# Two graph layers over an 8192 x 8192 adjacency: 89 of its 256 blocks multiplied with seven half-size products instead of eight, VectorE making the combinations of their quarters

## The reference

```
h = relu(layernorm(x));  x = x + adj @ (h * (u >= 0.1) / 0.9)
h = relu(layernorm(x));  x = x + adj @ (h @ W) + b
```

## Time and profile before

| what | value |
|---|---|
| median of three runs | 919.41 us |
| profiled execution, its own device time | 920.12 us |
| profiled execution, span of the page | 918.3 us |
| TensorE matmul busy | 900.0 us, 98% |
| VectorE busy | 234.5 us, 26% |
| GpSimd busy | 2.6 us |
| transfers | 363.53 MB, mean 396 GB/s |
| granted TensorE clock | full speed in every slice |

### The profile page before, as it was taken

The page is one execution under the profiler, slowest core; times in us unless marked ns, Lnnn a source line. Parts: engine busy times, 40 slices in busy tenths (PEclk is TensorE's granted clock), DMA queues, the critical chain, the costliest instruction groups (busy, mean ns, idle before and its releaser), DMA issues.

```text
span 918.3 us, 10443 instructions
## 1 busy us (share of the span) xinstructions
PE 900.0 (98%) x4488; PEld 415.4 (45%) x4488; DVE 234.5 (26%) x449; ACT 42.8 (5%) x120; POOL 2.6 (0%) x13
## 2 busy tenths in 40 slices
PE   6799999999999999999999999999999999999998
PEld 5445444444444444444444444444444444444443
DVE  5364732323203202030303021030220300300334
ACT  3100000000000000000000000000000000000000
POOL 1000000000000000000000000000000000000000
PEclk9999999999999999999999999999999999999999
DMA  8999999999999999999999999989999999999993
GB/s 348 421 420 420 422 420 422 420 421 421 421 420 421 420 421 420 421 419 421 403 419 379 410 367 380 399 339 369 385 353 382 371 386 419 390 390 389 412 422 149
DMA packets 52909, 363.53 MB, mean 396 GB/s; under 512 B 5728, under 2 KB 6016, under 8 KB 10752
## 3 DMA queue, kind: packets, MB, share of 16 engines
q1 hardware_dynamic: 52800, 362.83, 97.5%
q0 software_dynamic: 64, 0.03, 0.0%
HBM read 360.74 MB, written 2.10 MB: 395 GB/s over the span
## 4 chain that ended last, share of the span: by engine, by line
PE 92%; DMA 5%; SPq 2%; issue 0%; DVE 0%
PE banks L720 45%; PE row_sums L695 37%; PE banks L714 6%; DMA blocks<-in_adj 5%; PE banks L730 3%; SPq L464 1%; PE row_sums L704 1%; PE banks L807 0%; PE finished L772 0%; PE row_sums L772 0%; SPq L447 0%; SPq L446 0%; DVE x L654 0%
## 5 line engine op out<-in xcount | busy, mean ns | idle before, releaser
L720 PE MATMUL banks<-blocks,features 128*64 128x512 f32 x1912 | 665.2, 593 | 0.0
L695 PE MATMUL row_sums<-blocks,features 128*64 128x512 f32 x1696 | 547.1, 592 | 1.5 <-DMA blocks<-in_adj 1.5
L720 PEld LDWEIGHTS banks<-blocks,features 128*64 128x64 f32 x1912 | 221.3, 137 | 215.6 <-issue 215.1
L695 PEld LDWEIGHTS row_sums<-blocks,features 128*64 128x64 f32 x1696 | 192.7, 137 | 201.6 <-issue 196.4
L617 DVE TENSOR_TENSOR acc<-acc,banks 64x512 f32<-64x512 f32 (+1 forms) x112 | 76.8, 686 | 597.9 <-PE banks L720 540.7
L714 PE MATMUL banks<-blocks,features 128*64 128x512 f32 x224 | 98.1, 592 | 0.1
L524 ACT ACTIVATE turned<-finished 32x128 f32<-32x128 f32 (+1 forms) x68 | 17.8, 262 | 790.3 <-DVE finished L584 789.1
L730 PE MATMUL banks<-blocks,features 128*64 128x256 f32 x240 | 54.3, 379 | 0.1
L714 PEld LDWEIGHTS banks<-blocks,features 128*64 128x64 f32 x224 | 30.6, 137 | 29.0 <-issue 28.8
L730 PEld LDWEIGHTS banks<-blocks,features 128*64 128x64 f32 x240 | 32.8, 137 | 21.7 <-issue 8.5
L704 PE MATMUL row_sums<-blocks,features 128*64 128x256 f32 x256 | 30.5, 382 | 7.1 <-DMA blocks<-in_adj 7.1
(11 more groups left out here) (48 smaller groups left out, 97.0 us busy)
## 6 DMA issues: line engine op xcount, KB each, us to landing
blocks<-in_adj SPq DMA_DIRECT2D x339, 1024.0 KB, 13.0
out<-x SPq DMA_DIRECT2D x7, 256.0 KB, 3.6
x<-in_x SPq DMA_DIRECT2D x1, 1024.0 KB, 10.9
acc<-in_u SPq DMA_DIRECT2D x1, 1024.0 KB, 12.9
blocks<-in_adj SPq DMA_DIRECT2D x2, 512.0 KB, 25.1
x<-in_x SPq DMA_DIRECT2D x1, 768.0 KB, 7.2
acc<-in_u SPq DMA_DIRECT2D x1, 768.0 KB, 8.8
x<-in_x SPq DMA_DIRECT2D x1, 256.0 KB, 3.1
```

Of the source, the lines that this page charges most:

```text
L695: return nc.tensor.matmul(row_sums[at, t.unit % 2, nodes], features[:, tile_of(k, j), 0:D], tile, start=first and t.n == unit_first[t.unit ...
L720: return nc.tensor.matmul(banks[at, t.sum.bank, nodes], features[:, tile_of(t.k, j), D:2 * D], tile, start=t.n == t.sum.first and j == t.t ...
```

## The change

From row 4 on, a `both` item becomes a **seven**: 89 of the 92. The 512 x 512 block A is seen as four quarters (2 halves of its nodes x 2 halves of its tiles) and the features as B with two halves of tiles x two layers. The 2 x 2 product A B then takes seven products of quarters instead of eight (Winograd's form), each of 2 matmuls of 256 columns: 14 matmuls of 256 in place of 8 of 512.

For that, combinations must be made first. VectorE makes four of features (`mixed`, 128 x 128 elements each) and four of quarters of the block (`quarters`, 128 x 512 elements each; one of them, A11 - A21, is written over A21 in the block's own slot), eight subtractions or additions per block, in `make_quarters`. There are two sets of these buffers, so a block's combinations may start when the seven before the last is used, and are placed at most three items ahead. The products of a whole row add up in two further PSUM banks; when the row's last seven is done, `add_seven` adds them to `x1` and `acc` in seven additions where there was one. A unit's end now waits for these.

The rest follows from it. The PSUM tensor `finished` goes, and the transposes of a unit's end are put into `row_sums` instead, so the first item of unit m waits for the copies out of it. The ring has 15 slots in place of 16. Loads of a seven are issued as if they were needed two items sooner. `merged` gives each queue a window: sevens start 12 us after a unit's begin and end 8 us before its end, late items lie between 14 us after the begin and 30 us before the end. The late `both(k + 1, k)` is put ahead of the pairs in `late`. `x` and `u` come in two parts instead of three.

```
-SLOTS = 16
+SLOTS = 15
+SEVEN_FROM = 4
+SEVEN_LOAD, SEVEN_MADE, SEVEN_SETS = 2, 3, 2
+SUM_BANKS, SEVEN_BANKS = 4, 2
-STEP, BLOCK_LOAD, LANDING, MARGIN, H2_LEAD, ROW_LEAD = 0.858, 2.49, 1.6, 8.0, 8.0, 10.0
-PARTS = [(0, 1), (1, 4), (4, PAIRS)]
+STEP, BLOCK_LOAD, LANDING, MARGIN, H2_LEAD, SEVEN_OFF, LATE_OFF = 0.858, 2.49, 1.6, 8.0, 8.0, (12.0, 8.0), (14.0, 30.0)
+PARTS = [(0, PAIRS // 2), (PAIRS // 2, PAIRS)]
...
     def both(self, s, k):
-        return Item("both", [self.operand(s, k)], k, s, s + 1)
+
+        whole = s < SEVEN_FROM or (s, k) == (BLOCKS - 1, BLOCKS - 2)
+        return Item("both" if whole else "seven", [self.operand(s, k)], k, s, s + 1)
...
+    for n, t in enumerate(sevens):
+        t.nth, t.set = n, n % SEVEN_SETS
+        t.at = max(t.n - SEVEN_MADE, t.loads()[0].released, sevens[n - SEVEN_SETS].n if n >= SEVEN_SETS else 0)
...
+            def make_quarters(t):
...
+                dve.wait_ge(h2_ready, t.needs)
+                if t.nth >= SEVEN_SETS:
+                    dve.wait_ge(used, sevens[t.nth - SEVEN_SETS].n + 1)
+                nc.vector.tensor_tensor(t1, b12, b11, ALU.subtract).then_inc(seven_mixed, 1)
+                nc.vector.tensor_tensor(t3, b22, b12, ALU.subtract).then_inc(seven_mixed, 1)
+                dve.wait_ge(seven_mixed, 4 * t.nth + 1)
+                nc.vector.tensor_tensor(t2, b22, t1, ALU.subtract).then_inc(seven_mixed, 1)
+                dve.wait_ge(seven_mixed, 4 * t.nth + 3)
+                nc.vector.tensor_tensor(t4, b21, t2, ALU.subtract).then_inc(seven_mixed, 1)
+                s1, s2, s4 = (quarters[:, t.set, n, :, :] for n in range(3))
+                dve.wait_ge(block_arrived[t.loads()[0].slot], t.loads()[0].arrived)
+                nc.vector.tensor_tensor(s1, a21, a22, ALU.add).then_inc(seven_made, 1)
+
+                nc.vector.tensor_tensor(a21, a11, a21, ALU.subtract).then_inc(seven_made, 1)
+                dve.wait_ge(seven_made, 4 * t.nth + 1)
+                nc.vector.tensor_tensor(s2, s1, a11, ALU.subtract).then_inc(seven_made, 1)
+                dve.wait_ge(seven_made, 4 * t.nth + 3)
+                nc.vector.tensor_tensor(s4, a12, s2, ALU.subtract).then_inc(seven_made, 1)
...
+                pe.wait_ge(seven_mixed, 4 * t.nth + 4)
+                for j in range(2):
+                    product(A11_B11, a11, b11, j, first=True)
+                    of_layer_1(1, 1, a22, t4, j)
+                for j in range(2):
+                    of_layer_1(j, 0, a12, b21, j)
+                pe.wait_ge(seven_made, 4 * t.nth + 2)
+                for j in range(2):
+                    product(S1_T1, s1, t1, j, first=True)
+                    product(S3_T3, s3, t3, j, first=True)
+                pe.wait_ge(seven_made, 4 * t.nth + 4)
+                for j in range(2):
+                    product(S2_T2, s2, t2, j)
+                    done = product(S4_B22, s4, b22, j)
```

More of the change, by code:

```diff
@@ L80, in __init__, with merged @@
     def __init__(self, p, half, n):
-        self.p, self.half, self.first, self.ahead = p, half, n, None
+        self.p, self.half, self.first, self.ahead, self.seven = p, half, n, None, None
 def stays(i, k):
     return k <= i // 2 * 2 + 1 + KEPT
-def merged(queues, lead):
+def merged(queues, windows):
     total = sum(t.steps * STEP for q in queues for t in q)
@@ L96, in merged @@
                 continue
[L97 to L101, removed]
+            begin, end = windows[n][0], max(total - windows[n][1], windows[n][0] + 1.0)
+            if now < begin and any(d < len(r) and now >= w[0] for d, r, w in zip(done, queues, windows)):
+                continue
+            at = begin + (end - begin) * (done[n] + 0.5) / len(q)
             if best is None or at < best[0]:
@@ L149, in layer_2_of @@
             late[-1].k1 = other.k
+        if 0 < k < BLOCKS - 1:
+            late.append(self.both(k + 1, k))
         for p in range(PAIRS - 1, -1, -1):
@@ L229, in items @@
                 again = again[:max(0, int((0.97 * work - loads) / (2 * BLOCK_LOAD - 4 * STEP * 0.97)))]
-                items += merged([both, ones, again, late], ROW_LEAD)
+                items += merged([both, ones, again, late], [SEVEN_OFF, (0, 0), (0, 0), LATE_OFF])
             self.waiting = [w for w in self.waiting if w[1] not in again]
@@ L245, in plan @@
             load.until = n
+    sevens = [t for t in items if t.kind == "seven"]
+    loads.sort(key=lambda load: load.first - (SEVEN_LOAD if items[load.first].kind == "seven" else 0))
     free, holder, count = [-1] * SLOTS, [None] * SLOTS, [0] * SLOTS
-    for load in loads:
+    for n, load in enumerate(loads):
         load.slot = min(range(SLOTS), key=lambda q: free[q])
-        assert free[load.slot] < load.first, "a block needs a slot that is still held"
+        assert free[load.slot] < min(later.first for later in loads[n:]), "a block needs a slot that is still held"
         count[load.slot] += 1
@@ L259, in plan @@
             for half in range(2):
-                if t.kind == "one" or (t.kind == "both" and half != t.row % 2) or (t.kind == "mix" and half == 1):
+                if t.kind in ("one", "seven") or (t.kind == "both" and half != t.row % 2) \
+                        or (t.kind == "mix" and half == 1):
                     unit_items[t.unit][half].append(n)
-    unit_first = {m: [h[0] for h in halves] for m, halves in unit_items.items()}
-    unit_last = {m: [h[-1] for h in halves] for m, halves in unit_items.items()}
+    unit_first = {m: {half: h[0] for half, h in enumerate(halves) if h} for m, halves in unit_items.items()}
+    unit_last = {m: {half: h[-1] for half, h in enumerate(halves) if h} for m, halves in unit_items.items()}
+    unit_end = {max(t.n for t in items if t.unit == m): m for m in range(UNITS)}
     sums, row_sum = [], {}
@@ L302, in plan @@
         bank_free[q.bank], bank_of[q.bank] = q.last, q
-    unit_end = {max(last): m for m, last in unit_last.items()}
     pair_end = {}
@@ L308, in plan @@
     finals = sorted(range(PAIRS), key=lambda p: pair_end[p])
-    return items, loads, sums, ahead_done, unit_first, unit_last, unit_end, pair_end, finals
+    return items, loads, sums, sevens, ahead_done, seven_done, unit_first, unit_last, unit_end, pair_end, finals
 def bass_gnn(nc, x, adj, u, wb, out):
@@ L314, in bass_gnn @@
     ALU, ACT, AX = mybir.AluOpType, mybir.ActivationFunctionType, mybir.AxisListType
-    items, loads, sums, ahead_done, unit_first, unit_last, unit_end, pair_end, finals = plan()
+    (items, loads, sums, sevens, ahead_done, seven_done, unit_first, unit_last, unit_end, pair_end,
+     finals) = plan()
     closing = {q.last: q for q in sums}
@@ L658, in _ @@
                 if n in closing:
-                    add_sum(closing[n])
+                    (add_sum if closing[n].seven is None else add_seven)(closing[n])
+                for t in sevens:
+                    if t.at == n:
+                        make_quarters(t)
                 if n - 1 in unit_end:
```

148 lines of the change are left out of this document (106 added, 42 removed).

## The result

The changed kernel takes 905.52 us, median of 4 runs (903.23 to 906.49), against 919.47 us for the kernel before beside it: a ratio of 0.9841, 95% interval 0.9829 to 0.9853, 14 us less. The forecast was 893 us with a range of 883 to 908. So the direction and the range held, and nearly half of the forecast gain of 26 us is missing. (A slot of `blocks` is 8 KB per partition, 4 tiles of 512 fp32 numbers, and not the 16 KB stated above.)

A forecast was written before the change was run, and what follows sets the result against it. TensorE's work, 98% busy, was taken to bound the kernel. From 919.4 us, 28.2 us saved after 450 us gave 891.2; 2 us added for VectorE in runs of sevens made 893 us, range 883 to 908.

The forecast's parts named there:

- TensorE's work: In each seven: seven couples of 256-column matmuls take 3.02 us against 3.43, saving 36.4 us over 89 blocks.
- Up to unit 9's end the saving is lost: Units 5 to 9, transfers full: their 20 sevens' 8.2 us counted as lost to waits for blocks.
- above the floor, so this saving is paid in full: After 450 us: 69 sevens save 28.2 us, span ends at 890 us, above a transfer floor near 875.
- The fourth rival: After 450 us: transfers become the bound, no gain, chance 0.03; a part, blocks late, 3 to 5 us, 897, chance 0.08.
- the smaller ring: SyncE's loads issued behind a slot's release come late by one slot, 2.5 us, counted inside the 8.2 us.
- the forecast's own case: Whole kernel: 893 us, own range 885 to 898, chance 0.52.
- the first rival: VectorE's combinations run at full length, 4.18 us per seven: 10.5 us more, 902 us (898 to 906), chance 0.17.
- the second: TensorE runs dry at sevens' new waits, 0.22 us each time: 908 us, twice 923 (900 to 923), chance 0.12.
- VectorE: In make_quarters: eight operations overlap to 3.5 us per seven, VectorE about 70% busy; 2 us added for runs of sevens.
- TensorE empties at its new waits: At a seven's waits, though VectorE is in time: 0.22 us once each, 15 us over 69 sevens; chance 0.12.
- Slower by VectorE's operations on blocks: VectorE's operations on blocks cost more than any row shows: slower from 4.6 us per seven, 925 us and more; chance 0.08.
- The unit's end at nothing: Row's end additions (4.2 us) and the unit's own chain (6.3 us) cost nothing, as nobody waits before late begins.

The follow-up runs named there:

- e7: The changed kernel with its order and 15 slots, but all 92 blocks as boths with eight products and no combinations: 923.30 us.
- e2: The changed kernel with a ring of 14 slots in place of 15, nothing else: 934.86 us.
- e4: The changed kernel with loads of sevens issued in plain order of first use, not two items sooner: 896.47 us.
- e6: The changed kernel with 16 slots, room coming from two shared buffers, so the right value of one product is left out: 893.70 us.
- e9: The changed kernel, 15 slots, loads in plain order of first use and other windows for sevens and late items: 889.94 us.
- e10: The order of e9 with the 16 slots and two shared buffers of e6, one product's right value left out: 887.91 us.
- e5: The changed kernel with four more waits, so each of a seven's eight VectorE operations waits for the one before it: 910.61 us.
- e1: The changed kernel with VectorE's four combinations of quarters made for only 64 of their 512 elements: 902.74 us.

## Why the prediction was half right

- *TensorE's work.* 3.02 us per seven, 36.4 us in all: measured at 3.02. Right.
- *Up to unit 9's end the saving is lost.* 8.2 us forecast. Where unit 9 ends is told by ScalarE's operation of the earlier trace rows; in the change it is

```profile
439.16 0.30 ACT L585 ACTIVATE dev<-square,eps 128x4 f32<-128x4 f32 x1 [1.21 <-DVE square L652]
```

| kernel | slots | unit 9's end, us | from there to the end of the span, us |
|---|---|---|---|
| before | 16 | 447.5 | 470.9 |
| e7 (eight products) | 15 | 450.0 | 470.9 |
| the change | 15 | 439.2 | 464.2 |
| e2 | 14 | 444.1 | 489.9 |
| e4 | 15 | 438.8 | 456.2 |
| e6 | 16 | 439.2 | 453.1 |
| e9 | 15 | 437.7 | 450.8 |
| e10 | 16 | 437.8 | 448.6 |

  By unit 9's end the order of the sevens has done two pairs less than the kernel before (163 loads, not 167), 6.9 us of work. With nothing saved it would end at 440.6 us; it ended at 439.2, so 6.8 of the 8.2 us were lost. No order and no 16th slot of these runs brings it below 437.7. Right in mechanism and size.
- *"above the floor, so this saving is paid in full".* This is the step that failed. I set the bytes left after 450 us against the full rate and found a floor of 875 us, 15 us under the time so far. A floor from the mean rate says nothing on single blocks: the ring has 15 slots, the late blocks landed 7.3 to 10.2 us after issue, and the order gave some of them 5.2 us. Beyond unit 9's end the sum gives 470.9 + 6.9 - 28.2 = 449.6 us; measured are 464.2, so 14.6 of the 28.2 us were not paid. TensorE stood still for 9.2 us more than before from 450 us to the end, and two stretches at half clock cost 2 x 1.7 us; some 2 us are not placed. The fourth rival named it ("a block late here and there") and undersized it, at 3 to 5 us. I had put the smaller ring into 2.5 us inside the 8.2, where e2 and e6 show 29 and 12 us per slot. That the ring, the order and the early loads make the loss is shown: each was changed by itself (the ring in e2 and e6, the loads in e4, the order in e9 against e4), and e9 brings this part to 450.8 us. How the rest divides between the order and the sevens' pace is not shown beyond what e7 says.
- *The range.* It held by width and not by its reasons. 905.5 lies outside the 885 to 898 of the forecast's own case and above the fourth rival's 895 to 902. It lies in the ranges of the first rival (898 to 906) and the second (900 to 923), and neither of these happened: the time alone would have pointed to the wrong cause.
- *VectorE.* Pitch 3.50 forecast, 3.48 measured; waits of TensorE for it 0.8 us, 2 us allowed, and at the end of unit 16 as said. The rival at full length was priced at 10.5 us, 9 of it above the forecast; by hand (e5) it is 5 us on top of the late blocks. Right, but for some 4 us that e1 leaves open.
- *TensorE empties at its new waits.* A seven without late operands runs in 3.02 us; the rival is out.
- *Slower by VectorE's operations on blocks.* They last 684 to 692 ns; out.
- *The unit's end at nothing.* TensorE's wait for features written there was 1.0 us, once. Right.

What stays open: how the 7.3 to 10.2 us from issue to landing divide into waiting behind other loads and the block's own transfer; how much of the run-to-run spread of the change (3.3 us; the kernel before had 0.5 us beside it and 4.4 us beside e1 to e4) is the clock; and the 4 us of e1.

## What to carry to other kernels

A floor of bytes by the mean rate is necessary and not sufficient: in a ring, ask of each load which item frees its slot and how much work lies between that item and the use, and hold it against the time from issue to landing, not against the pitch. When a change makes the consumer faster, that distance shrinks, and one slot or an "earlier" load, which holds a slot longer, can cost more than the new work: 12 us and 9 us here, against 3 to 4 us that came back with most of VectorE's (e1). Keep items with two loads apart in the order, and price a wait of TensorE with the clock that it may cost after it.

## What the runs showed that I had not expected

- Issuing loads earlier made blocks later: 9 us (e4).
- A wait of 2.3 us and one of 3.5 us of TensorE were each followed by a stretch at half clock of 3.4 us; the wait of 3.0 us that ended near 255 us was followed by none in the change (clock 1.00), and by one in e1 and e6 (0.60 from 254.4 to 258.2 us in e1, 0.67 from 254.9 to 258.5 in e6). So the length of the wait alone doesn't decide.
- One slot beside fifteen: 29 us lost with 14, 12 us won with 16, and nothing between 15 and 16 in the kernel before.
